# Two-layer decoder: query and key halves stacked along the contraction, by way of device memory and a ring in SBUF

## The reference, cut to what matters

| k | attention | head width | keys | what is special |
|---|---|---|---|---|
| 0 | splat | 16 | 256 | query and key halves are exponentials of squared distances |
| 1 | cross0 | 16 | 120 | keys come from a context of 120 tokens |
| 2 | causal | 16 | 256 | masked, queries and keys have a bias |
| 3 | self1 | 32 | 256 | a mask after the softmax |
| 4 | cross1 | 32 | 120 | context keys |

```python
scores = q @ k.T * s          # q: 256 x width, k: keys x width
p = softmax(scores)           # over the keys
out = p @ v
```

## Time and profile before

### The profile page before, as it was taken

The page is one execution under the profiler, slowest core; times in us unless marked ns, Lnnn a source line. Parts: engine busy times, 40 slices in busy tenths (PEclk is TensorE's granted clock), DMA queues, the critical chain, the costliest instruction groups (busy, mean ns, idle before and its releaser), DMA issues. The chain is left out here.

```text
span 3842.1 us, 94561 instructions
## 1 busy us (share of the span) xinstructions
PE 3304.1 (86%) x38960; PEld 2345.7 (61%) x38960; DVE 2753.4 (72%) x6299; ACT 2095.4 (55%) x4222; POOL 976.8 (25%) x1792
## 2 busy tenths in 40 slices
PE   2989888889888888888988888899988898988886
PEld 1666666666665656666656666576655665666664
DVE  6777776777766767777767677677776777777755
ACT  5645655555456564564465555545555555466552
POOL 1312341122223321231133122212342122124310
PEclk9899998999989999999989898899988998999987
DMA  5000000000000000000000000000000000000000
GB/s 168 3 3 2 2 3 5 10 8 3 2 2 4 5 3 7 7 3 2 7 2 2 5 4 8 6 4 2 2 2 3 10 10 4 2 2 2 2 4 6
DMA packets 30365, 31.49 MB, mean 8 GB/s; under 512 B 8673, under 2 KB 26482, under 8 KB 29938
## 3 DMA queue, kind: packets, MB, share of 16 engines
q1 hardware_dynamic: 29938, 25.44, 2.2%
HBM read 21.24 MB, written 4.19 MB: 7 GB/s over the span
## 5 line engine op out<-in xcount | busy, mean ns | idle before, releaser
L1142 ACT ACTIVATE p<-bank,p_log 128x512 f32<-128x512 f32 (+2 forms) x1280 | 747.6, 584 | 1238.8 <-PE bank L834 1188.6
L1716 POOL TENSOR_TENSOR prob<-p,prob 120x256 f16<-120x256 f32 (+2 forms) x512 | 453.3, 885 | 1734.7 <-ACT prob L1143 1733.5
L1143 ACT ACTIVATE prob<-bank,p_log 128x512 f16<-128x512 f32 (+2 forms) x1280 | 748.2, 585 | 0.0
L1418 DVE TENSOR_REDUCE negm<-bank 128x2 f16<-128x512 f32 (+1 forms) x1280 | 675.5, 569 | 26.7 <-PE bank L789 15.6
L1336 DVE TENSOR_TENSOR prob<-p,prob 128x512 f16<-128x512 f32 (+2 forms) x768 | 467.4, 616 | 179.4 <-ACT prob L1143 175.7
L811 PE MATMUL bank<-q,k 32*128 32x256 f16 (+2 forms) x6144 | 491.0, 286 | 70.8 <-ACT prob L1143 28.0
L701 PE MATMUL bank<-w_exp,ident_h 128*128 128x512 f16 x1280 | 425.2, 417 | 16.6 <-DVE xa L1330 12.2
L1725 POOL TENSOR_SCALAR_AFFINE_SELECT probm<-prob 128x128 f16<-128x128 f16 x1024 | 328.1, 359 | 314.9 <-DVE prob L1336 314.9
L811 PEld LDWEIGHTS bank<-q,k 32*128 32x128 f16 (+1 forms) x6144 | 305.1, 109 | 150.2 <-issue 42.0
L834 PE MATMUL bank<-ident_h,negm 128*128 128x256 f16 (+2 forms) x2560 | 379.8, 270 | 0.0
L1708 POOL TENSOR_TENSOR rstd<-veps,minus_half 128x2 f32<-128x2 f32 (+2 forms) x192 | 146.3, 762 | 809.8 <-DVE veps L1304 809.1
(11 more groups left out here) (300 smaller groups left out, 6223.5 us busy)
## 6 DMA issues: line engine op xcount, KB each, us to landing
x<-in_x SPq DMA_DIRECT2D x16, 256.0 KB, 2.6
out<-z SPq DMA_DIRECT2D x16, 256.0 KB, 2.1
x<-in_li SPq DMA_DIRECT2D x7, 256.0 KB, 4.5
xa<-in_li SPq DMA_DIRECT2D x7, 256.0 KB, 4.5
z<-in_li SPq DMA_DIRECT2D x6, 256.0 KB, 4.6
x<-in_wq SPq DMA_DIRECT2D x4, 256.0 KB, 4.4
cx<-in_ctx_t SPq DMA_DIRECT2D x16, 60.0 KB, 1.8
cx<-in_ctx SPq DMA_DIRECT2D x16, 60.0 KB, 1.8
```

The lines of the kernel that those rows point to most:

```text
L1142: act(p32[0:n, g % PBUF32, 0:cols], ps[0:n, 0:cols], ACT.Exp, bias=p_log[0:n, :], scale=a.scale)
L1143: act(prob[0:n, 0, g % PBUF, 0:cols], ps[0:n, 0:cols], ACT.Exp, bias=p_log[0:n, :], scale=a.scale).then_inc(a_done, one(a_done))
L1418: v.tensor_reduce(negm[:, h * NT:(h + 1) * NT], ring_v[bank_of(e, v_full)][:, :].rearrange("p (t n) -> p t n", t=NT)[:, :, 0:ATTNS[k].keys ...
L1716: g.tensor_tensor(prob[0:n, 1, m % PBUF, 0:cols], p32[0:n, m % PBUF32, 0:cols], prob[0:n, 0, m % PBUF, 0:cols], ALU.subtract).then_inc(pp_ ...
```

## The change

The halves of a head are now laid along the contraction, so that one matmul makes the sum of the partial products: for width 32 the rows of a head are q high, q low, q high against k high, k high, k low (three planes, 96 rows), for width 16 four planes (64 rows, low·low among them) and 16 rows of zeros (80 rows). Both `row_scores` and `exact_scores` use these operands.

Since the planes of a head have to come to lie under each other on the partitions, they go through device memory. ScalarE and VectorE write high and low into one tile `made` of [128, 2, 4, 256], which queries and keys share, and which there is once. SP stores each plane (`store`), 3 or 4 DMAs for the queries of a phase and as many for its keys, into `q_heads` and `k_heads` in DRAM. It fills (`fill`) a ring of three slots with them, four heads (a quad) to a slot, two DMAs a quad, four quads a phase. New waits: ScalarE (VectorE for splat) waits with the keys' halves until the queries of the same phase are stored (`stored_ahead`), and with the queries until the keys of the phase before are; a fill waits until the keys are stored and until the quad three before it was used; TensorE waits at the first head of a quad for its slot. The two sets of `qT` and `kT` go, and so do the doubled keys with `parity`. Keys of cross0 are now made like the others (`lows` out of the bank), and ScalarE writes the keys' high half of causal as well.

In `exact_scores` the heads of a pair now come one after the other, and the wait for a row maximum stands behind the score products of its head rather than ahead of those of the pair. In `row_scores` they come one after the other as well.

```diff
+QUAD, QUADS, SLOTS = 4, 4, 3
+Q_PLANES = (0, 1, 0, 1)
+K_PLANES = {3: (0, 0, 1), 4: (0, 0, 1, 1)}
...
-    def at(self, h):
-        if self.dim == 32:
-            return h // 4, 32 * (h % 4), h // 4
-        return h // 8, 32 * ((h % 8) // 2), 2 * (h % 2) + h // 8
+        self.planes = 3 if dim == 32 else 4
+        self.stacked = 96 if dim == 32 else 80
+        self.together = P // dim
...
-ORDER = [(k, b, h) for k, b in PHASES for h in heads_of(ATTNS[k])]
+ORDER = [(k, b, h) for k, b in PHASES for h in range(HEADS)]
...
+def stored_ahead(k, b, what):
+    if what == "k":
+        return STORED[k, b, "q"]
+    p = PHASE[k, b]
+    return STORED[(*PHASES[p - 1], "k")] if p > 0 else 0
+def slot_filled(quad):
+    return 2 * 16 * (quad // SLOTS + 1)
...
-        qT = [pair(f"q{s}", 4, TOK) for s in range(SETS)]
-        kT = [pair(f"k{s}", 4, TOK) for s in range(SETS)]
+        made = pair("made", 4, TOK)
+        q_ring, k_ring = (sb(f"{what}_ring", [96, SLOTS, QUAD, TOK], F16) for what in "qk")
+        heads16 = {what: nc.dram_tensor(f"{what}_heads16", (2, 8, 80, 2, TOK), F16).ap() for what in "qk"}
+        heads32 = {what: nc.dram_tensor(f"{what}_heads32", (2, 4, 96, 4, TOK), F16).ap() for what in "qk"}
...
+                def operands(g):
+                    a, h = ATTNS[ORDER[g][0]], ORDER[g][2]
+                    slot_of, at = g // QUAD % SLOTS, h % QUAD
+                    return q_ring[0:a.stacked, slot_of, at, :], k_ring[0:a.stacked, slot_of, at, 0:a.keys]
                 def row_scores(pair):
 
-                    k, b, h = ORDER[pair[0]]
-                    a, s = ATTNS[k], PHASE[k, b] % SETS
-                    if h == 0:
-                        e.wait_ge(*was_split("k", k, b))
-                    banks = [slot("v", "max", pair[0])]
-                    stream(banks[0], STREAM_ROWS)
-                    banks.append(slot("v", "max", pair[1]))
-                    for i in range(NT):
-                        n = P if a.causal and i == 0 else a.keys
-                        for g, ps in zip(pair, banks):
-                            t, q0, kx = a.at(ORDER[g][2])
-                            last = mm(ps[:, i * TOK:i * TOK + n], qT[s][q0:q0 + 32, 0, t, i * P:i * P + P],
-                                      kT[s][q0:q0 + 32, 0, kx, 0:n], start=i == 0, stop=i == NT - 1 and not a.causal)
-                            if i == NT - 1 and not a.causal:
-                                last.then_inc(v_full, one(v_full))
-                    if a.causal:
-                        for ps in banks:
+                    for g in pair:
+                        a = ATTNS[ORDER[g][0]]
+                        if g % QUAD == 0:
+                            e.wait_ge(ring_full[g // QUAD % SLOTS], slot_filled(g // QUAD))
+                        q, kk = operands(g)
+                        ps = slot("v", "max", g)
+                        if g == pair[0]:
+                            stream(ps, STREAM_ROWS)
+                        for i in range(NT):
+                            n = P if a.causal and i == 0 else a.keys
+                            last = mm(ps[:, i * TOK:i * TOK + n], q[:, i * P:i * P + P], kk[:, 0:n],
+                                      start=i == 0, stop=i == NT - 1 and not a.causal)
+                        if a.causal:
                             for c in (0, P):
                                 mm(ps[:, c:c + P], ident_h[:, :], mask_q[:, c:c + P], start=False, stop=False)
-                            mm(ps[:, TOK + P:2 * TOK], ident_h[:, :], mask_q[:, 0:P], start=False, stop=True
-                               ).then_inc(v_full, one(v_full))
+                            last = mm(ps[:, TOK + P:2 * TOK], ident_h[:, :], mask_q[:, 0:P], start=False, stop=True)
+                        last.then_inc(v_full, one(v_full))
 
                 def exact_scores(pair):
 
-                    k, b, _ = ORDER[pair[0]]
-                    a, s = ATTNS[k], PHASE[k, b] % SETS
-                    banks = [slot("a", "p", g) for g in pair]
-                    e.wait_ge(*moved("max", pair[-1]))
-                    for j, (k0, n) in enumerate(a.key_tiles):
-                        i0 = j * P if a.causal else 0
-                        for kp, qp in PARTS:
-                            for g, ps in zip(pair, banks):
-                                t, q0, kx = a.at(ORDER[g][2])
-                                mm(ps[0:n, j * TOK:j * TOK + TOK - i0], kT[s][q0:q0 + 32, kp, kx, k0:k0 + n],
-                                   qT[s][q0:q0 + 32, qp, t, i0:TOK],
-                                   start=(j, kp, qp) == (0, 0, 0), stop=False)
-                    n = a.key_tiles[0][1]
-                    for g, ps in zip(pair, banks):
-                        h = ORDER[g][2]
+                    for g in pair:
+                        a, h = ATTNS[ORDER[g][0]], ORDER[g][2]
+                        q, kk = operands(g)
+                        ps = slot("a", "p", g)
+                        for j, (k0, n) in enumerate(a.key_tiles):
+                            i0 = j * P if a.causal else 0
+                            mm(ps[0:n, j * TOK:j * TOK + TOK - i0], kk[:, k0:k0 + n], q[:, i0:TOK],
+                               start=j == 0, stop=False)
+                        e.wait_ge(*moved("max", g))
+                        n = a.key_tiles[0][1]
                         rows = ps[0:n, :].rearrange("p (j c) -> p j c", j=NT)
...
+                        if g % QUAD == QUAD - 1:
+                            freed["ring", g // QUAD] = a_full, sent(a_full)
...
-                            direct = not a.causal and (a.dim == 32 or what == "q")
                             feature_major(w, col, a.tiles, source, n, tok, what, k, b,
-                                          by="dve" if direct else "act", low=("xT", k, b) if what == "q" else None)
+                                          by="act" if a.causal else "dve", low=("xT", k, b) if what == "q" else None)
...
-                        if a.causal:
-                            raw_tiles(a.tiles, TOK, qT[s], bq2[:, 0:2])
-                        else:
-                            for m in range(0, a.tiles, 2):
-                                highs((qT[s][:, 0, m:m + 2, :], two, 1 / W_SCALE))
-                        yield
-                        if a.dim == 32:
-                            for m in range(0, a.tiles, 2):
-                                highs((kT[s][:, 0, m:m + 2, 0:a.keys], lambda ps: two(ps)[:, :, 0:a.keys],
-                                       1 / W_SCALE))
-                        else:
-                            raw_tiles(a.tiles, a.keys, None, bq2[:, 2:4] if a.causal else None)
-                        yield
+                        for what, n, bias in (("q", TOK, bq2[:, 0:2]), ("k", a.keys, bq2[:, 2:4])):
+                            if stored_ahead(k, b, what) > 0:
+                                e.wait_ge(stored, stored_ahead(k, b, what))
+                            if a.causal:
+                                raw_tiles(a.tiles, n, made, bias)
+                            else:
+                                for m in range(0, a.tiles, 2):
+                                    highs((made[:, 0, m:m + 2, 0:n], lambda ps: two(ps)[:, :, 0:n], 1 / W_SCALE))
+                            yield
...
+                def split_heads(a, what, k, b):
+                    n = a.keys if what == "k" else TOK
+                    if not a.splat and not a.causal:
                         for m in range(0, a.tiles, 2):
+                            lows(made[:, 1, m:m + 2, 0:n], made[:, 0, m:m + 2, 0:n],
                                  lambda ps: ps[:, :].rearrange("p (t n) -> p t n", t=2)[:, :, 0:n], 1 / W_SCALE)
                         return
+                    at = next_half(what, k, b)
+                    tiles = raw[:, at:at + a.tiles, 0:n]
+                    if a.causal:
+                        last = low_part(made[:, 1, 0:a.tiles, 0:n], tiles, made[:, 0, 0:a.tiles, 0:n])
+                    else:
+                        if stored_ahead(k, b, what) > 0:
+                            e.wait_ge(stored, stored_ahead(k, b, what))
+                        if what == "q":
+                            last = split(tiles, made[:, 0, 0:a.tiles, :], made[:, 1, 0:a.tiles, :])
+                        else:
                             for t in range(KT):
+                                last = split(raw[:, at + t, 0:n], made[:, 0, t, 0:n], made[:, 1, t, 0:n],
+                                             k_scale[:, t:t + 1])
                     last.then_inc(split_done, one(split_done))
...
+                def store(what, k, b):
+                    a, p = ATTNS[k], PHASE[k, b]
+                    e.wait_ge(*was_split(what, k, b))
+                    if p >= 2 and what == "q":
+                        for quad in range((p - 2) * QUADS, (p - 1) * QUADS):
+                            e.wait_ge(ring_full[quad % SLOTS], slot_filled(quad))
```

(24 more changed lines are left out.)

70 lines of the change are left out of this document (27 added, 43 removed).

## The result

| | before | after |
|---|---|---|
| median of the runs, us | 3836.4 (4 runs, 3827.1 to 3843.6) | 4107.6 (4 runs, 4104.3 to 4108.4) |
| ratio, 95% interval | | 1.069 (1.067 to 1.072) |
| span of the profiled execution, us | 3842.1 | 4102.6 |

The change makes the kernel 7% slower: 271 us, where 157 were forecast. (The profiled spans differ by 261 us; they are single executions.) First the clock, the busy times behind the start-up and the page's busy times, after the change; they answer to the earlier trace rows.

The account below looks back on a forecast made before the run. TensorE was taken to bound most of the time, chains of small VectorE and GpSimd steps the rest. 3842 − 142 − 10 + 279 + 30 = 3999, less 6 to the median: 3993 us, range 3830 to 4150 us.

Parts of the forecast that it names:

- TensorE's saving: Score products on TensorE: stacking saves 203 us of work over splat, self1, cross and causal pairs, taken as −142 us.
- The 70%: Share of TensorE's 203 us saving expected to shorten the run, the rest becoming longer waiting; gives −142 us.
- −10: VectorE without the doubled keys: some 60 us less busy, counted as −10 us (0 to −30) since it is not the bound.
- Price of a store and a fill: DMAs through device memory: width-32 store 10.7 us, width-16 store 4.4 us, fills 2.8 us and 2.3 us for cross0.
- Upper end: Store price with one engine per destination block, 4 or 8 engines: 10.7 us for width 32, 4.4 us for width 16.
- The new waits: Waits for stored queries and keys and filled slots, by kind of phase: together 328 us, taken as +279 us.
- the 85%: Share of the 328 us of new waits that counts, as other late work arrives during them; gives +279 us.
- The 42 waits of ScalarE: Sign of being right: ScalarE's keys wait for a DMA, 5 us or so each, in 42 phases.
- the twelve of TensorE: Sign of being right: twelve waits of TensorE ahead of its filler L725, 5 to 15 us each.
- The clock: TensorE's granted clock falls behind some 48 new waits: 0 to 160 us, taken as +30 us.
- Rival 1: Stores use all 16 engines, taking 3.6 and 2.9 us; the kernel gets faster, 3757 us; chance 0.15.
- Rivals 2 and 3: 2: ScalarE's waits hidden, 3881 us, chance 0.11; 3: low clock halves saving, 4199 us, mean clock below 0.87, chance 0.08.

Follow-up runs that it names:

- e3: Kernel before, with every pair's 32-row products put on rows 0 to 63 instead of taking turns with rows 64 to 127; 3862.1 us, 1.007 of before.
- e4: The change without stores and fills: stacked products read one static ring slot filled once with weights times 0.125; 3629.5 us, 0.949 of before.
- e2: The change with all stores but splat's reshaped, row within a head outermost, to run on 16 engines; 3833.7 us, 1.000 of before.
- e10: e4 with every score product reading only the first 32 of its 80 or 96 rows; 3867.7 us, 1.007 of before.
- e1: The change without stores and fills: stacked products read one static ring slot filled once with zeros; 3626.3 us, 0.946 of before.
- e7: The change with separate tiles and semaphores for made queries and keys, and two ring slots for three; 3880.6 us, 1.015 of before.
- e5: e4 plus all the change's stores and fills, into places nobody reads, with no engine but SyncE waiting for them; 3635.2 us.

## Why the prediction was right or wrong

The sign, the mechanism and the range held; the size was 115 us short (4107.6 for 3993), and just outside the 3900 to 4100 that the forecast called its own. Step by step:

- **TensorE's saving (203 us of work, −142 net).** The work fell by 122 us. Summed over all score steps at full clock it is: the switch ahead of the pair 62 us (0.09 for each of 640, as forecast), causal 30 (with the switches 41, forecast 42), cross 31 (with 23: 54, forecast 87), splat 13 and self1 0 (with 23: 36, forecast 74). That makes 136; TensorE's other products took some 14 more. What failed is taking one pair of the earlier trace rows and one of the earlier trace rows for all: both were slow ones. Of 92 undisturbed pairs of 256 keys 47 had more products side by side (e3) and only 12 took about as long as the earlier trace rows or longer; from the filler to the values the 92 took 0.09 us more in the mean than the pairs after the change, not 0.29. Pairs of 120 keys took 1.31 before and 1.09 after (medians), 0.22 less and not 0.34. Products after the change do start 0.109 us apart, as named. The 70% for work that would turn into waiting was wrong too: e4 shows 9 us of added idle time. A saving too large by 81 and a discount too large by 61 nearly cancelled; that −142 came near −122 is luck. VectorE's busy time fell by the 58 us that were forecast as 60, but no part of the time can be put down to its −10.
- **Price of a store and a fill.** Upper end right: 11.3 and 5.0 us for 10.7 and 4.4, on 4 and 8 engines. The two or three issues of 0.6 us between the first and the last DMA of a store were left out. Fills, both DMAs together, took 2.9 us for cross0 and 3.5 for self1 (medians), for 2.3 and 2.8. With 16 engines the stores took 3.7 and 4.3 us for 3.6 and 2.9: a width-16 store of four DMAs hardly gains; the time between its first and its last issue alone is 1.9 us.
- **The new waits (328 us, times 85%).** This step failed most. Added idle time of TensorE by what is made during a phase (from its first row scores to those of the next), measured against forecast: self1 of `LATE_SOON` 121 (114), the other 26 width-32 phases 127 (120), cross0 by `LATE` 31 (34), cross0 of `LATE_SOON` 58 (42), the rest with the start-up 20 (18): 356 in all, against 328. The terms were right to a tenth or so, but for the late cross0, and the 85% was not: the idle time grew by more than the full sum, so no discount was due. That step alone put the net 77 us too low, the largest part of the miss. The 42 waits of ScalarE of 5 us or so came as 48 with 337 us in total, 7 each, the twelve of TensorE as 19 with 121 us.
- **The clock (+30).** Measured +27, by luck, as a sum of two things: −114 for the stacked form (e4 against before), which the forecast doesn't have, and +140 for the round trip (after against e4), of which the 30 are less than a quarter. The 3.3 us for each wait in its upper end isn't what the earlier trace rows gives either: of 9.75 us of busy time at a clock of 0.51 half is lost, 4.8.
- **Rival 1** had its condition tested by e2. With 16 engines the time is 3834, not 3757: its waits were priced at 80 us and are 147 (685 − 538). The twelve late phases cost more than 4.8 and 3.9 us each, namely 6.9 and 8.7 of idle time: the chain of self1 takes 14.5 us where it was 7.8, that of cross0 13.7 for 4.95.
- **Rivals 2 and 3.** ScalarE's waits were not hidden: 127 us of idle in those phases. The mean clock was 0.884, above the 0.87 named for rival 3.

In sum: stacking −213 where the forecast had −152, the round trip +473 where it had +309. The two errors, 61 and 164 us, have opposite signs, so the total looks better than its terms.

## What to carry to other kernels

What a round trip through device memory cost here is its waits (473 us) and not its traffic (6 us). Look at the outermost dimension of both sides of each DMA first (here 11.3 or 3.7 us for the same bytes), then at what may not be overwritten until it has landed, then at the slots. Measure one pair in several places before multiplying it by 640, and don't take a share off a sum of waits without a row that shows what fills them. Where a kernel is often at the lower clock, look there for a second price or gain of a change of TensorE's form; here it was as large as the saved work (−114 beside −108).

## What the runs showed of the hardware that was not expected

- The granted clock went with how TensorE works, and not only with whether it does. Same number of products, same order: 96 or 80 rows, 15% idle, mean clock 0.936 (e4); 32 rows, 9% idle, mean clock 0.894 (e10). Rows and switches between the forms are not separated. Stacked operands of zeros or of weights made no difference (both 0.936, e1 and e4).
- 32-row products of neighbouring steps ran four abreast without being written so, where their rows differ: 16 in 0.77 us (before); with all pairs on the same rows 81 of 93 undisturbed pairs took 1.4 us and none 1.2 (e3).
- Two stores of three DMAs on 4 engines each, under way together, took about as long as one after the other: 19.0 us (e7).
- 202 MB of stores and fills beside the work cost about 6 us in 3630, although each store used a quarter or half of the engines (e5).
